# One inverse root of the norms for both halves of an image, and new places for the loop's steps, in a vision tower on Trainium2

## The chip, the cores and the metric

The kernel runs on one core of a Trainium2 chip. The metric is the device time of one execution in microseconds (us). The engines are TensorE (PE, with its weight loads as PEld), VectorE (DVE), ScalarE (ACT), GpSimd (POOL) and SyncE (SP), which here does nothing but issue DMA transfers. Each engine works through its own list of instructions strictly in order; between engines there are only semaphores.

## The reference, cut to what matters

Sixteen images of 3 x 256 x 256 go through three stages. A normalised 31 x 31 correlation gives 256 tokens of width 256 for each image, then comes causal attention and then a feed-forward part. The change lies in the attention:

```python
q = (x @ Wq).reshape(b, n, QH, DH).transpose(0, 2, 1, 3)        # QH = 16, DH = 64
k = kv[..., :H * DH].reshape(b, n, H, DH).transpose(0, 2, 1, 3) # H = 8
def _l2norm(x):
    n = jnp.maximum(jnp.linalg.norm(x, axis=-1, keepdims=True), 1e-12)
    return x / n
q = _mh_rmsnorm(q, q_gamma)       # _l2norm(q) * gamma
k = _mh_rmsnorm(k, k_gamma)
sim = jnp.einsum('bhgid,bhjd->bhgij', q, k)
sim = jnp.tanh(sim / SOFTCLAMP) * SOFTCLAMP * DH ** (-0.5)
attn = jax.nn.softmax(jnp.where(causal, neg, sim), axis=-1)
out = jnp.einsum('bhgij,bhjd->bhid', attn, v) @ Wout
```

So every token has 24 norms to be inverted in an image: 16 of queries and 8 of keys. A token sits in a partition; the 256 tokens of an image are two halves ("tb" 0 and 1) of 128.

## The kernel before

The three stages are three blocks, one after another, with a meeting of all engines between them: `token_stage`, `attention_stage`, `mlp_stage`. The attention works on 4 groups of 4 images (`GROUPS`, `GI`). Three groups are iterations of a loop in the program (`BODY`), the last is written out behind it (`FINAL`). The queries and keys of the very first image are made at the end of the token stage (`FIRST`, by `first_parts`), and each group makes those of the first image of the next group near its end (`EDGE_AT`).

The work of a group is a list of steps, `attention_order`. Each step has a place in a table, a number whose unit is one head: head n of the group's 32 has its score at place n. The list is sorted by place, and every engine takes from it, in that order, its own share of each step. The tables are `IMAGE_AT` (for an image, relative to the place at which its heads begin), `EDGE_AT`, `GROUP_AT` and the three constants under them. The steps that matter:

- **make** (0 to 7): one of eight projections of an image. PE does six matmuls into one of four PSUM banks (`job`); ACT copies queries and keys to `raw` (L924) and values to `v` (L928). 0 to 2 are the queries and keys of half 0, 4 to 6 of half 1; 3 and 7 are values.
- **square** (ACT, L936): squares the 1536 columns of a half into `squares`, which the profile calls `lines`. There is one such buffer, so the square of half 1 waits until the sum of half 0 has read it.
- **sum** (DVE, L990): 1536 squares to 24 norms in `rn`.
- **root** (DVE, L996 to L1011): clip, a first guess from the bits, three Newton steps of three instructions: eleven instructions on 128 x 24.
- **scale** (DVE, L1018): multiplies 1536 columns by the inverse norms.
- **turn** (0, 1, 2, 4, 5, 6): PE transposes scaled queries or keys (L1123), ACT writes the fp16 high part (L945, L949), and **low** is DVE's low part (L1027, L1032). A turn of half 0 waits for scale 0.
- **score** (PE L1136; ACT tanh L955 and exp L958; POOL mask L888). The tile `sim` holds one head, so the score of head n on PE waits for the tanh of head n-1 on ACT.
- **mix** (PE L1151, DVE L1040 to L1048), two heads and a half behind the score; **turn_o**, **project** and **norm** (DVE L1064 to L1080) end a group; **turn_h** and the **rms** steps prepare the tokens of the next group.
- **bits** (DVE, L1053): ORs a chunk of the feed-forward weights, `words`, 704 columns of int32, into `bits`, to learn which of two multiplication routes these weights allow. A group has eight chunks and two bits steps for each image. There is one buffer `words`: SP fetches the next chunk when the bits step of the last one is done.

SP's list in a group, in which every transfer stands behind the ones above it:

```python
sp.wait_ge(at.s_job, run.jobs_before(g))                       # BODY only
sp.dma_start(at.hn[:], rows(g + 1)).then_inc(at.s_hn, 16)      # lines<-tokens
for c in range(CHUNKS):
    if c == 1:
        sp.wait_ge(at.s_store, g * 32 + 32)
        sp.dma_start(h[:], rows(g)).then_inc(at.s_h, 16)
    sp.wait_ge(at.s_bits, g * CHUNKS + c + 1)
    sp.dma_start(at.words[:], WORDS[...]).then_inc(at.s_words, 16)
sp.wait_ge(at.s_x1, g + 1)                                     # after norm, BODY only
for half in range(2):
    sp.dma_start(X1[g * 2 + half], h[...]).then_inc(at.s_store, 16)
```

Of the kernel before, what the change touches and what calls it, by code (L numbers as in the profile page):

```python
# [8 lines left out]
I32 = mybir.dt.int32  # L9
ALU = mybir.AluOpType  # L10
# [29 lines left out]
ROOT_SEED = float(0x5F3759DF)  # L40
# [2 lines left out]
EPS_LN = 1e-5  # L43
W3 = QH * DH + 2 * HEADS * DH
QK = QH * DH + HEADS * DH
ROOTS = 1
BANKS = 4
WH = W3 // 2
WPARTS = [(half, f) for half in range(2) for f in range(FB)]
# [5 lines left out]
class Shared:  # L55


    def __init__(self, nc, ctx):
# [21 lines left out]
        def gone(name, shape, dt=F32):  # L80
            with nc.sbuf_tensor(name, shape, dt, side="right") as early:
                return early
# [18 lines left out]
        self.rn = sb("rn", [P, 2, QK // DH])  # L101
        self.guess = sb("guess_b", [P, ROOTS * (QK // DH)])
        self.slope = sb("slope_b", [P, ROOTS * (QK // DH)])
        sb("x_second_end", [P, plane - HEADS * TOK - (2 + 2 * ROOTS) * (QK // DH)])
        self.dump_first = gone("dump_first", [P, PR, D])
# [58 lines left out]
def token_stage(nc, sh, at, X, XT, TF, TPAD, H, WORDS, WEIGHTS, WQKV, NW, GQ, GK):  # L164
# [533 lines left out]
NH = GI * HEADS  # L698
LAG = 2
IMAGE_AT = {  # L700
    ("make", 0): -8, ("make", 1): -8, ("make", 2): -7.725, ("square", 0): -7.18, ("make", 6): -6.997,
    ("sum", 0): -6.79, ("root", 0): -6.361, ("make", 4): -6.348, ("scale", 0): -6.321, ("make", 5): -5.839,
    ("make", 3): -5.512, ("square", 1): -5.39, ("sum", 1): -5.219, ("turn", 0): -4.545, ("make", 7): -4.423,
    ("root", 1): -4.413, ("low", 0): -4.389, ("turn", 1): -3.147, ("scale", 1): -2.767, ("low", 1): -2.619,
    ("turn", 2): -2.538, ("low", 2): -1.89, ("turn", 4): -1.49, ("low", 4): -1.23, ("turn", 5): -1.205,
    ("turn", 6): -1.068, ("low", 5): -1.063, ("low", 6): -0.99,
}
EDGE_AT = {
    ("make", 0): -8, ("make", 1): -8, ("make", 2): -8, ("square", 0): -7.718, ("make", 6): -6.743,
    ("sum", 0): -6.311, ("make", 4): -5.808, ("root", 0): -5.602, ("scale", 0): -5.343, ("make", 5): -4.841,  # L710
    ("square", 1): -4.533, ("make", 3): -3.75, ("sum", 1): -3.523, ("root", 1): -2.958, ("make", 7): -2.776,
    ("scale", 1): -1.653, ("turn", 0): -0.263, ("low", 0): 0.74, ("turn", 1): 1.01, ("turn", 2): 2.113,
    ("low", 1): 2.862, ("low", 2): 3.052, ("turn", 4): 3.86, ("low", 4): 4.18, ("turn", 5): 4.291,
    ("turn", 6): 4.697, ("low", 5): 4.751, ("low", 6): 4.828,
}
GROUP_AT = {
    ("rms_sum", 0): 4, ("rms_sum", 1): 6, ("rms_sum", 2): 8.635, ("rms_sum", 3): 15.072, ("turn_h", 0): 19.823,
    ("turn_h", 1): 19.97, ("turn_h", 2): 20.742, ("turn_h", 3): 21.416, ("project", 0): 36.821,
    ("project", 1): 37.209, ("project", 2): 37.906, ("project", 3): 38,
}  # L720
GROUP_AT.update({("rms_root", 0): 15.489, ("rms_scale", 0): 16.649, ("norm", 0): 38.109})
MIX_AT, TURN_O_AT, BITS_AT = LAG + 0.502, (1.332, 2.286), (2.334, 7.379)


def first_parts():

    tokens = [("turn_h", k) for k in range(4)]
    makes = [("make", 0, j) for j in (0, 1, 2)] + [("square", 0, 0), ("sum", 0, 0), ("root", 0, 0)]
    makes += [("make", 0, j) for j in (4, 5, 6)] + [("square", 0, 1), ("scale", 0, 0), ("sum", 0, 1), ("root", 0, 1)]
    makes += [("make", 0, j) for j in (3, 7)] + [("scale", 0, 1)]  # L730
    turns = [[(kind, 0, 4 * tb + r) for r in range(3) for kind in ("turn", "low")] for tb in range(2)]
    return {"tokens": tokens, "makes": makes, "turns": turns}
# [57 lines left out]


FIRST_PARTS = first_parts()
FIRST = Stretch(FIRST_PARTS["tokens"] + FIRST_PARTS["makes"] + FIRST_PARTS["turns"][0] + FIRST_PARTS["turns"][1], False, 0)
BODY = Stretch(attention_order(False), True, 1)
# [10 lines left out]
class Attention:  # L805
# [162 lines left out]
    def vector_steps(self, dve, run, g, steps):  # L968
# [4 lines left out]
        for step in steps:  # L973
# [13 lines left out]
            elif kind == "sum":  # L987
                tb = step[2]
# [1 line left out]
                dve.reduce_sum(self.rn[:, tb], self.squares[:, 0:QK].rearrange("p (h d) -> p h d", d=DH), AX_X)\  # L990
                   .then_inc(self.s_ss, 1)
            elif kind == "root":
                tb = step[2]
                t = self.image(g, step[1]) * 2 + tb
                dve.wait_ge(self.s_ss, t + 2)
                dve.tensor_scalar(self.rn[:, tb], self.rn[:, tb], 1e-24, None, ALU.max).then_inc(self.s_clip, 1)  # L996
                dve.wait_ge(self.s_clip, t + 1)
                dve.tensor_scalar(self.guess[:].bitcast(I32), self.rn[:, tb].bitcast(I32), -0.5, ROOT_SEED,
                                  ALU.mult, ALU.add).then_inc(self.s_guess, 1)
                for k in range(NEWTON):  # L1000
                    dve.wait_ge(self.s_guess, t * NEWTON + k + 1)
                    dve.tensor_tensor(self.slope[:], self.guess[:], self.guess[:], ALU.mult).then_inc(self.s_slope, 1)
                    dve.wait_ge(self.s_slope, (t * NEWTON + k) * 2 + 1)
                    dve.scalar_tensor_tensor(out=self.slope[:], in0=self.slope[:], scalar=-0.5, in1=self.rn[:, tb],
                                             op0=ALU.mult, op1=ALU.mult).then_inc(self.s_slope, 1)
                    dve.wait_ge(self.s_slope, (t * NEWTON + k) * 2 + 2)
                    if k < NEWTON - 1:
                        dve.scalar_tensor_tensor(out=self.guess[:], in0=self.slope[:], scalar=1.5, in1=self.guess[:],
                                                 op0=ALU.add, op1=ALU.mult).then_inc(self.s_guess, 1)
                    else:  # L1010
                        dve.scalar_tensor_tensor(out=self.rn[:, tb], in0=self.slope[:], scalar=1.5, in1=self.guess[:],  # L1011
                                                 op0=ALU.add, op1=ALU.mult).then_inc(self.s_rn, 1)
            elif kind == "scale":
                tb = step[2]
                dve.wait_ge(self.s_rn, self.image(g, step[1]) * 2 + tb + 1)
                heads = self.raw[:, tb].rearrange("p (h d) -> p h d", d=DH)
                by = self.rn[:, tb].rearrange("p (h d) -> p h d", d=1).to_broadcast([P, QH + HEADS, DH])
                dve.tensor_tensor(heads, heads, by, ALU.mult).then_inc(self.s_qn, 1)  # L1018
            elif kind == "low":
                img, tb, r = step[1], step[2] // 4, step[2] % 4  # L1020
# [3 lines left out]
                if r < 2:  # L1024
                    for e in range(4):
                        u = 4 * r + e
                        ins = dve.scalar_tensor_tensor(out=self.q_lo[:, img % 2, u, cols], in0=bank[:, e * P:(e + 1) * P],  # L1027
                                                       scalar=self.gamma[:, u:u + 1], in1=self.q_hi[:, img % 2, u, cols],
                                                       op0=ALU.mult, op1=ALU.subtract)
                    ins.then_inc(self.s_emptied["queries"], 1)  # L1030
                else:
                    dve.scalar_tensor_tensor(out=self.k_lo[:, img % 2, :, cols], in0=bank.rearrange("p (h t) -> p h t", t=P),  # L1032
                                             scalar=KEY_SCALE, in1=self.k_hi[:, img % 2, :, cols],
# [659 lines left out]
```

## Time and profile before

| | |
|---|---|
| median of 3 runs | 1805.04 us (1791.48 to 1810.17) |
| profiled execution, its own time | 1788.73 us |
| its span | 1786.9 us |
| PE busy | 1726.3 us, 97% |
| DVE busy | 1137.2 us, 64% |
| ACT busy | 930.3 us, 52% |
| POOL busy | 427.8 us, 24% |

The span is from the first to the last instruction of the profiled execution; its own time has 1.8 us around that. The first and last of the three plain runs differ by 18.7 us, so a difference of about 1% is what a measurement of this kernel can tell from none. A busy share is an average over the three stages: the token stage ends at about 536 us of the span, the attention lies from 537 to 1112 us, and the feed-forward part follows. A clock column (PEclk) gives the clock granted to TensorE as a share of 2.4 GHz; 0.50 is 1.2 GHz.

### The profile page before, as it was taken

The page shows a single profiled execution, that of the slowest core. Times are in us where ns is not written, and L with a number is a line of the kernel's source. Part 1 is how long each engine was busy: PE and PEld are TensorE (multiplying, and loading weights), DVE is VectorE, ACT ScalarE, POOL GpSimd, SP SyncE. Part 2 cuts the span into 40 slices and gives each one's busy share as a digit, 9 for nine tenths or more (in the row PEclk, how much of TensorE's full clock was granted, in tenths as well). Part 3 has the DMA queues.
Part 4 walks back from the last instruction along what each step waited for, and adds up shares of the span by engine and source line. Part 5 has one row for each costly group of instructions (what it writes and reads, how often), then busy time and mean ns, then how long its engine had stood idle before and what let it go on. Part 6 is the DMA issues. An engine that isn't in the chain of part 4 may idle for free. (4 is left out here: it accounts for less than half of the span.)

```text
span 1786.9 us, 33009 instructions
## 1 busy us (share of the span) xinstructions
PE 1726.3 (97%) x12152; PEld 1509.7 (84%) x12152; DVE 1137.2 (64%) x2191; ACT 930.3 (52%) x1309; POOL 427.8 (24%) x515
## 2 busy tenths in 40 slices
PE   5999999999999999999999998999999999999998
PEld 5999998999987887888888887788888888888886
DVE  7899898898996877786877884423324141515242
ACT  8655555566658985895995994222222222222221
POOL 2000000000112222221222321434344333434343
PEclk9999999999999999999999999999999999999999
DMA  6322222223103002001100203600000000000000
GB/s 195 111 89 85 113 79 111 86 78 143 48 1 108 26 18 89 26 26 71 36 26 9 81 18 112 214 1 24 25 1 24 1 25 1 24 1 24 1 13 13
DMA packets 26421, 97.23 MB, mean 54 GB/s; under 512 B 3081, under 2 KB 11401, under 8 KB 21010
## 3 DMA queue, kind: packets, MB, share of 16 engines
q1 hardware_dynamic: 26258, 94.96, 15.5%
q8 instruction: 115, 1.88, 0.4%
q14 instruction: 48, 0.39, 0.1%
HBM read 82.33 MB, written 24.15 MB: 60 GB/s over the span
## 5 line engine op out<-in xcount | busy, mean ns | idle before, releaser
L658 PE MATMUL conv<-w,x 128*128 128x368 f16 (+5 forms) x3960 | 452.7, 277 | 3.8 <-issue 3.8
L658 PEld LDWEIGHTS conv<-w,x 128*128 128x128 f16 x3960 | 427.2, 146 | 27.9 <-issue 4.5
L1439 ACT ACTIVATE raw_c<-ring,sh 128x512 f32<-128x512 f32 x128 | 87.6, 689 | 334.3 <-PE ring L1542 334.2
L1451 DVE CAST ha_hi<-raw_c 128x512 fp32r<-128x512 f32 x128 | 85.2, 665 | 201.0 <-ACT raw_c L1439 198.8
L888 POOL TENSOR_SCALAR_AFFINE_SELECT probs<-probs 128x256 f32<-128x256 f32 x256 | 129.9, 530 | 342.2 <-ACT probs L958 342.2
L1398 POOL TENSOR_TENSOR ha_lo<-raw_c,ha_hi 128x512 fp32r<-128x512 f32 x128 | 165.3, 1291 | 189.5 <-DVE ha_hi L1451 189.5
L1542 PE MATMUL ring<-ha_hi,wh 128*128 128x512 f32 x512 | 199.4, 389 | 0.9 <-POOL ha_lo L1398 0.9
L1542 PE MATMUL ring<-ha_lo,wh 128*128 128x512 f32 x512 | 199.2, 389 | 0.0
L1542 PE MATMUL ring<-hb_lo,wh 128*128 128x512 f32 x512 | 199.2, 389 | 0.0
L1542 PE MATMUL ring<-hb_hi,wh 128*128 128x512 f32 x512 | 199.2, 389 | 0.0
L1151 PEld LDWEIGHTS mixed<-v,probs 128*128 128x128 f32 x1536 | 185.5, 193 | 10.7 <-POOL probs L888 1.7
L1151 PE MATMUL mixed<-v,probs 128*128 128x65 f32 x1536 | 192.2, 275 | 1.9 <-DVE o L1044 1.8
L1451 DVE CAST hb_hi<-raw_c 128x512 fp32r<-128x512 f32 x64 | 35.7, 558 | 187.3 <-ACT raw_c L1439 187.0
L379 ACT ACTIVATE lines<-job 128x512 f32<-128x512 f32 x96 | 50.0, 605 | 167.8 <-PE job L638 167.7
L955 ACT ACTIVATE probs<-sim,span 128x768 f32<-128x768 f32 x128 | 115.8, 905 | 12.6 <-PE sim L1136 12.0
L472 DVE TENSOR_TENSOR_SCAN box<-lines 128x271 f32<-128x271 f32 x192 | 120.2, 699 | 3.5 <-ACT lines L379 3.5
L1114 PE MATMUL job<-wqkv_hi,ht_hi 128*128 128x512 f32 x256 | 110.5, 432 | 7.6 <-PEq L171 3.6
L1398 POOL TENSOR_TENSOR hb_lo<-raw_c,hb_hi 128x512 fp32r<-128x512 f32 x64 | 82.5, 1290 | 140.5 <-DVE hb_hi L1451 140.5
L1542 PEld LDWEIGHTS ring<-ha_hi,wh 128*128 128x128 f32 x512 | 96.1, 188 | 21.6 <-POOL ha_lo L1398 1.6
L1542 PEld LDWEIGHTS ring<-hb_lo,wh 128*128 128x128 f32 x512 | 96.1, 188 | 20.0
L1542 PEld LDWEIGHTS ring<-ha_lo,wh 128*128 128x128 f32 x512 | 96.1, 188 | 19.9
L1542 PEld LDWEIGHTS ring<-hb_hi,wh 128*128 128x128 f32 x512 | 96.1, 188 | 19.9
(161 smaller groups left out, 3198.5 us busy)
## 6 DMA issues: line engine op xcount, KB each, us to landing
xt<-x_columns_in SPq DMA_DIRECT2D x12, 1163.0 KB, 5.2
xp<-x_patches_in SPq DMA_DIRECT2D x12, 1152.0 KB, 5.1
hidden_words<-hidden_weights_in SPq DMA_DIRECT2D x8, 1408.0 KB, 8.5
words<-hidden_words SPq DMA_DIRECT2D x32, 352.0 KB, 3.0
wh<-hidden_words SPq DMA_DIRECT2D x8, 1024.0 KB, 10.0
tokens<-planes SPq DMA_DIRECT2D x4, 1024.0 KB, 4.6
h<-tokens SPq DMA_DIRECT2D x4, 1024.0 KB, 7.3
attended<-h SPq DMA_DIRECT2D x8, 512.0 KB, 3.5
```

The costliest lines, as they stand in the source:

```text
L379: act.activation(dst, turn[:, k % 4], ACT.Copy).then_inc(s_across, 1)
L472: return dve.tensor_tensor_scan(out, line[:, TH:TH + SCAN], line[:, 0:SCAN], 0.0, ALU.add, ALU.subtract)
L658: ins = pe.matmul(out, xs[:, c, RI - 1 - i:RI - 1 - i + NR, :, x].rearrange("p r g -> p (r g)"), w, start=(t == 0), stop=(t == size - 1), ...
L888: ins = pool.affine_select(out=diag, in_=diag, compare_op=ALU.is_ge, fill=0.0, base=0, pattern=[[0, 2], [1, P]], channel_multiplier=-1)
L955: act.activation(self.probs[:, n % 4], self.sim[:, :, 0:3 * P], ACT.Tanh, scale=self.span[:, 2:3]).then_inc(self.s_tanh, 1)
L1114: ins = pe.matmul(bank, x[:, f, img % GI, P * tb:P * tb + P], w[:, f, 512 * r:512 * r + 512], start=(t == 0), stop=(t == len(terms) - 1))
L1151: ins = pe.matmul(out, self.probs[:, n % 4, m, at:at + P], self.v[:, img % 2, jb, 2 * (hd // 2) + m], start=(jb == 0), stop=(jb == ib), sk ...
L1398: pool.tensor_tensor(dst[1][:, u % KH], raw[:, u % 4], dst[0][:, u % KH].bitcast(F32), ALU.subtract).then_inc(s_lo, 1)
L1439: act.activation(raw[:, u % 4], bank, ACT.Gelu, scale=scale[:, m:m + 1]).then_inc(s_gelu, 1)
L1451: dve.tensor_copy(dst[0][:, u % KH], raw[:, u % 4]).then_inc(s_hi, 1)
L1542: ins = pe.matmul(bank, a, b, start=start, stop=False, skip_group_check=True)
```

## The change

Two things are changed. First, the root is taken once for an image, on 48 norms, after the sums of both halves, where it was taken twice on 24. `guess` and `slope` are twice as wide (`ROOTS = 2`), `scale` of either half waits for that one root, and the two columns of `rn` are read as one. Second, the tables of places are new, as is the order in `first_parts`.

```diff
-ROOTS = 1
+ROOTS = 2
...
 IMAGE_AT = {
...
-    ("sum", 0): -6.79, ("root", 0): -6.361, ("make", 4): -6.348, ("scale", 0): -6.321, ("make", 5): -5.839,
...
+    ("make", 3): -5.898, ("root", 0): -5.788, ("make", 7): -5.749, ("scale", 0): -5.689, ("scale", 1): -4.382,
...
-MIX_AT, TURN_O_AT, BITS_AT = LAG + 0.502, (1.332, 2.286), (2.334, 7.379)
+MIX_AT, TURN_O_AT, BITS_AT = LAG + 0.95, (2.679, 3), (0.625, 1.427)
...
-    makes = [("make", 0, j) for j in (0, 1, 2)] + [("square", 0, 0), ("sum", 0, 0), ("root", 0, 0)]
-    makes += [("make", 0, j) for j in (4, 5, 6)] + [("square", 0, 1), ("scale", 0, 0), ("sum", 0, 1), ("root", 0, 1)]
+    makes = [("make", 0, j) for j in (0, 1, 2)] + [("square", 0, 0), ("sum", 0, 0)]
+    makes += [("make", 0, j) for j in (4, 5, 6)] + [("square", 0, 1), ("sum", 0, 1), ("root", 0, 0), ("scale", 0, 0)]
...
             elif kind == "root":
-                tb = step[2]
-                t = self.image(g, step[1]) * 2 + tb
-                dve.wait_ge(self.s_ss, t + 2)
-                dve.tensor_scalar(self.rn[:, tb], self.rn[:, tb], 1e-24, None, ALU.max).then_inc(self.s_clip, 1)
+                t = self.image(g, step[1])
+                norms = self.rn[:].rearrange("p b h -> p (b h)")
+                dve.wait_ge(self.s_ss, 2 * t + 3)
+                dve.tensor_scalar(norms, norms, 1e-24, None, ALU.max).then_inc(self.s_clip, 1)
...
             elif kind == "scale":
                 tb = step[2]
-                dve.wait_ge(self.s_rn, self.image(g, step[1]) * 2 + tb + 1)
+                dve.wait_ge(self.s_rn, self.image(g, step[1]) + 1)
```

The two bits steps of an image stood at 2.334 and 7.379 behind the start of its heads, and now stand at 0.625 and 1.427. Three places show what becomes of the lists.

On DVE, from the norm that ends a group (L1080) into the next group, before. In a row, `b_words` is the semaphore of a landed chunk, `b_sq` of a square, `b_ss` of a sum, `b_rn` of a root, `b_mix` of a mix on PE.

```order
L1080 TENSOR_SCALAR h<-h,moments_b,rstd_b 128x256 x7
...
L990 TENSOR_REDUCE rn<-lines 128x24 [waits b_sq]
L996 TENSOR_SCALAR rn<-rn 128x24 [waits b_ss]
L998 TENSOR_SCALAR guess_b<-rn 128x24 [waits b_clip]
...
L1011 SCALAR_TENSOR_TENSOR rn<-slope_b,guess_b 128x24 [waits b_slope]
L1018 TENSOR_TENSOR raw<-raw,rn 128x1536 [waits b_rn]
L1053 TENSOR_TENSOR bits<-bits,words 128x704 [waits b_bits,b_words]
L1040 RECIPROCAL rl<-mixed 128x4 [waits b_mix]
```

The same place on DVE now.

```order
L1080 TENSOR_SCALAR h<-h,moments_b,rstd_b 128x256 x7
...
L1053 TENSOR_TENSOR bits<-bits,words 128x704 [waits b_bits,b_words]
L990 TENSOR_REDUCE rn<-lines 128x24 [waits b_sq]
L1053 TENSOR_TENSOR bits<-bits,words 128x704 [waits b_bits,b_words]
L990 TENSOR_REDUCE rn<-lines 128x24 [waits b_sq]
L996 TENSOR_SCALAR rn<-rn 128x48 [waits b_ss]
...
L1011 SCALAR_TENSOR_TENSOR rn<-slope_b,guess_b 128x48 [waits b_slope]
L1018 TENSOR_TENSOR raw<-raw,rn 128x1536 [waits b_rn]
L1040 RECIPROCAL rl<-mixed 128x4 [waits b_mix]
```

The first bits step moved from behind the first scale to the very front, ahead of the first sum; the second, which stood five heads later, is between the two sums.

On ACT, at the start of a group, from the first square to the tanh of the fourth head, before. L924 and L928 are the copies of makes, `b_emptied_act` counts them.

```order
L936 ACTIVATE lines<-raw 128x1536 [waits b_ss,b_emptied_act]
L955 ACTIVATE probs<-sim,span 128x768 [waits b_mix,b_score]
L958 ACTIVATE probs<-probs 128x768 [waits b_tanh]
L924 ACTIVATE raw<-job 128x512 [waits b_job] x2
L955 ACTIVATE probs<-sim,span 128x768 [waits b_mix,b_score]
L958 ACTIVATE probs<-probs 128x768 [waits b_tanh]
L924 ACTIVATE raw<-job 128x512 [waits b_job]
L928 ACTIVATE v<-job 128x8x64 [waits b_mix,b_job]
L936 ACTIVATE lines<-raw 128x1536 [waits b_ss,b_emptied_act]
L955 ACTIVATE probs<-sim,span 128x768 [waits b_mix,b_score]
```

The same place on ACT now.

```order
L936 ACTIVATE lines<-raw 128x1536 [waits b_ss,b_emptied_act]
L955 ACTIVATE probs<-sim,span 128x768 [waits b_mix,b_score]
L958 ACTIVATE probs<-probs 128x768 [waits b_tanh]
L924 ACTIVATE raw<-job 128x512 [waits b_job] x3
L936 ACTIVATE lines<-raw 128x1536 [waits b_ss,b_emptied_act]
L955 ACTIVATE probs<-sim,span 128x768 [waits b_mix,b_score]
L958 ACTIVATE probs<-probs 128x768 [waits b_tanh]
L928 ACTIVATE v<-job 128x8x64 [waits b_mix,b_job] x2
```

The second square moved ahead of the tanh of the third head; before it stood ahead of that of the fourth.

On PE, behind the first mix of a group, now. `b_qn` is the semaphore of a scale.

```order
L1151 MATMUL mixed<-v,probs 128x65 [waits b_mixread,b_mask]
...
L1136 MATMUL sim<-q_hi,k_hi 128x256 [waits b_tanh]
...
L1151 MATMUL mixed<-v,probs 128x65 [waits b_mixread,b_mask]
...
L1136 MATMUL sim<-q_hi,k_hi 128x256 [waits b_tanh]
...
L1123 MATMUL job<-ident,raw 128x128 [waits b_qn,b_emptied_act]
```

All eight makes and three scores now stand ahead of this first mix, and the first turn behind the score of the fifth head; before, seven makes and three scores stood ahead of it, and the first turn behind the score of the fourth head, with one make still to come.

## Rows read from the trace of the kernel before

**Rows 1.** Busy time by stretch: start:end, length, PE, PEld, DVE, ACT, POOL, PEclk.

```profile
541.00:1106.00 565.00, 550.87 (x4561) 469.93 (x4560) 424.05 (x1140) 451.43 (x768) 142.14 (x269) 0.99 0.14 47
696.00:716.00 20.00, 18.65 (x161) 16.42 (x159) 16.99 (x46) 17.34 (x40) 5.92 (x10) 0.83 0.31 115
```

**Rows 2.** Waits of PE, 541 to 1106: total us, times, longest.

```profile
PE mixed L1151 <- DVE o L1044: 1.8, 2, 1.4
```

**Rows 3.** Groups of DVE, 541 to 1106: count, busy us, mean ns, idle before.

```profile
L1018 DVE TENSOR_TENSOR raw<-raw,rn 128x1536 f32<-128x1536 f32 x30 | 53.3, 1777 | 0.4
L990 DVE TENSOR_REDUCE rn<-lines 128x24 f32<-128x1536 f32 x30 | 52.5, 1749 | 16.6 <-ACT lines L936 16.4
L1053 DVE TENSOR_TENSOR bits<-bits,words 128x704 int32<-128x704 int32 x32 | 30.9, 964 | 3.6 <-DMA words<-hidden_words 3.6
...
L1002 DVE TENSOR_TENSOR slope_b<-guess_b 128x24 f32<-128x24 f32 x90 | 17.3, 193 | 3.1
```

**Rows 4.** Timeline of PE, second group: start us, length us, idle before.

```profile
683.99 0.50 PE L1114 MATMUL job<-wqkv_hi,ht_hi 128*128 128x512 f32 x1 [0.96 <-DVE h L1064]
...
696.14 1.45 PE L1151 MATMUL mixed<-v,probs 128*128 128x65 f32 x12
...
699.88 0.48 PE L1114 MATMUL job<-wqkv_hi,ht_hi 128*128 128x512 f32 x1
...
701.45 0.28 PE L1136 MATMUL sim<-q_hi,k_hi 64*128 64x256 f16 x2
...
702.04 1.55 PE L1151 MATMUL mixed<-v,probs 128*128 128x65 f32 x12
...
708.51 2.79 PE L1151 MATMUL mixed<-v,probs 128*128 128x65 f32 x12 [1.35 <-DVE o L1044]
```

**Rows 5.** Timeline of DVE at the start of the second group.

```profile
687.59 2.77 DVE L1080 TENSOR_SCALAR h<-h,moments_b,rstd_b 128x256 f32<-128x256 f32 x8 [2.25 <-POOL rstd_b L896]
...
700.02 0.89 DVE L1053 TENSOR_TENSOR bits<-bits,words 128x704 int32<-128x704 int32 x1 [2.21 <-DMA words<-hidden_words]
```

**Rows 6.** Timeline of SP's DMA issues at the start of the second group.

```profile
692.15 0.35 SPq L1192 DMA_DIRECT2D lines<-tokens  x1
692.90 0.59 SPq L1198 DMA_DIRECT2D words<-hidden_words  x1
695.10 0.33 SPq L1196 DMA_DIRECT2D h<-tokens  x1
701.08 0.33 SPq L1198 DMA_DIRECT2D words<-hidden_words  x1
```

**Rows 7.** Tile words, the chunk issued at 701.1: issue to landing, us.

```profile
DMA to landing us min/median/max: 3.1/3.1/3.1
```

**Rows 8.** Timeline of ACT, second group: the second square and the tanh behind it.

```profile
696.92 1.48 ACT L936 ACTIVATE lines<-raw 128x1536 f32<-128x1536 f32 x1
698.31 0.90 ACT L955 ACTIVATE probs<-sim,span 128x768 f32<-128x768 f32 x1
```

**Rows 9.** Timeline of PE, the first make of the third group.

```profile
833.23 0.49 PE L1114 MATMUL job<-wqkv_hi,ht_hi 128*128 128x512 f32 x1 [0.96 <-DVE h L1064]
```

**Rows 10.** Timeline of DVE, the first bits step of the third group.

```profile
848.44 0.89 DVE L1053 TENSOR_TENSOR bits<-bits,words 128x704 int32<-128x704 int32 x1 [1.36 <-DMA words<-hidden_words]
```

**Rows 11.** Timeline of PE, the first make of the last group.

```profile
978.75 0.47 PE L1114 MATMUL job<-wqkv_hi,ht_hi 128*128 128x512 f32 x1 [0.83 <-issue]
```

**Rows 12.** Tile words, 986.0 to 987.5: the last group's first chunk.

```profile
L1198 SPq DMA_DIRECT2D words<-hidden_words x1: 557/557/557, 986.6 to 986.6; - x1
...
DMA to landing us min/median/max: 4.4/4.4/4.4
```

**Rows 13.** Tile words, 542 to 543: the first group's first chunk.

```profile
L1198 SPq DMA_DIRECT2D words<-hidden_words x1: 347/347/347, 542.3 to 542.3; - x1
...
DMA to landing us min/median/max: 5.2/5.2/5.2
```

**Rows 14.** Timeline of PE, the first mix of the first group.

```profile
551.46 1.45 PE L1151 MATMUL mixed<-v,probs 128*128 128x65 f32 x12
```

More of the change, by code:

```diff
@@ L700 @@
 IMAGE_AT = {
-    ("make", 0): -8, ("make", 1): -8, ("make", 2): -7.725, ("square", 0): -7.18, ("make", 6): -6.997,
-    ("sum", 0): -6.79, ("root", 0): -6.361, ("make", 4): -6.348, ("scale", 0): -6.321, ("make", 5): -5.839,
-    ("make", 3): -5.512, ("square", 1): -5.39, ("sum", 1): -5.219, ("turn", 0): -4.545, ("make", 7): -4.423,
-    ("root", 1): -4.413, ("low", 0): -4.389, ("turn", 1): -3.147, ("scale", 1): -2.767, ("low", 1): -2.619,
-    ("turn", 2): -2.538, ("low", 2): -1.89, ("turn", 4): -1.49, ("low", 4): -1.23, ("turn", 5): -1.205,
@@ L706 @@
-    ("turn", 6): -1.068, ("low", 5): -1.063, ("low", 6): -0.99,
+    ("make", 0): -8, ("make", 2): -8, ("make", 1): -7.639, ("square", 0): -7.258, ("sum", 0): -7.065,
+    ("make", 6): -6.738, ("make", 4): -6.591, ("make", 5): -6.54, ("square", 1): -6.092, ("sum", 1): -5.91,
+    ("make", 3): -5.898, ("root", 0): -5.788, ("make", 7): -5.749, ("scale", 0): -5.689, ("scale", 1): -4.382,
+    ("turn", 0): -3.293, ("turn", 1): -3.106, ("low", 0): -3.002, ("low", 1): -2.585, ("turn", 2): -2.355,
+    ("turn", 4): -1.801, ("low", 2): -1.411, ("turn", 5): -1.099, ("turn", 6): -1.007, ("low", 4): -0.728,
@@ L707 @@
+    ("low", 5): -0.393, ("low", 6): -0.2,
 }
 EDGE_AT = {
[L709 to L713, printed above, removed]
@@ L714 @@
-    ("turn", 6): 4.697, ("low", 5): 4.751, ("low", 6): 4.828,
+    ("make", 0): -8, ("make", 1): -8, ("make", 6): -8, ("make", 2): -6.838, ("square", 0): -6.773, ("sum", 0): -6.15,
+    ("make", 4): -5.871, ("make", 5): -5.426, ("square", 1): -5.408, ("sum", 1): -4.903, ("root", 0): -4.559,
+    ("make", 3): -4.296, ("scale", 0): -3.515, ("make", 7): -2.169, ("scale", 1): -2.126, ("turn", 0): -0.473,
+    ("turn", 1): 1.494, ("low", 0): 1.678, ("low", 1): 2.558, ("turn", 2): 3.339, ("low", 2): 3.65,
@@ L715 @@
+    ("turn", 4): 4.546, ("low", 4): 4.554, ("turn", 5): 4.868, ("low", 5): 5.007, ("turn", 6): 5.041,
+    ("low", 6): 5.165,
 }
 GROUP_AT = {
-    ("rms_sum", 0): 4, ("rms_sum", 1): 6, ("rms_sum", 2): 8.635, ("rms_sum", 3): 15.072, ("turn_h", 0): 19.823,
-    ("turn_h", 1): 19.97, ("turn_h", 2): 20.742, ("turn_h", 3): 21.416, ("project", 0): 36.821,
-    ("project", 1): 37.209, ("project", 2): 37.906, ("project", 3): 38,
-}
-GROUP_AT.update({("rms_root", 0): 15.489, ("rms_scale", 0): 16.649, ("norm", 0): 38.109})
@@ L722 @@
-MIX_AT, TURN_O_AT, BITS_AT = LAG + 0.502, (1.332, 2.286), (2.334, 7.379)
+    ("rms_sum", 0): 3.791, ("rms_sum", 1): 8.365, ("rms_sum", 2): 9.606, ("rms_sum", 3): 15.392,
+    ("turn_h", 0): 18.316, ("turn_h", 1): 18.429, ("turn_h", 2): 20.558, ("turn_h", 3): 21.624,
+    ("project", 0): 37.164, ("project", 1): 37.193, ("project", 2): 37.217, ("project", 3): 38,
+}
+GROUP_AT.update({("rms_root", 0): 15.642, ("rms_scale", 0): 16.459, ("norm", 0): 38.343})
+MIX_AT, TURN_O_AT, BITS_AT = LAG + 0.95, (2.679, 3), (0.625, 1.427)
@@ L992, in vector_steps @@
             elif kind == "root":
-                tb = step[2]
-                t = self.image(g, step[1]) * 2 + tb
-                dve.wait_ge(self.s_ss, t + 2)
-                dve.tensor_scalar(self.rn[:, tb], self.rn[:, tb], 1e-24, None, ALU.max).then_inc(self.s_clip, 1)
+                t = self.image(g, step[1])
+                norms = self.rn[:].rearrange("p b h -> p (b h)")
+                dve.wait_ge(self.s_ss, 2 * t + 3)
+                dve.tensor_scalar(norms, norms, 1e-24, None, ALU.max).then_inc(self.s_clip, 1)
                 dve.wait_ge(self.s_clip, t + 1)
-                dve.tensor_scalar(self.guess[:].bitcast(I32), self.rn[:, tb].bitcast(I32), -0.5, ROOT_SEED,
+                dve.tensor_scalar(self.guess[:].bitcast(I32), norms.bitcast(I32), -0.5, ROOT_SEED,
                                   ALU.mult, ALU.add).then_inc(self.s_guess, 1)
@@ L1003, in vector_steps @@
                     dve.wait_ge(self.s_slope, (t * NEWTON + k) * 2 + 1)
-                    dve.scalar_tensor_tensor(out=self.slope[:], in0=self.slope[:], scalar=-0.5, in1=self.rn[:, tb],
+                    dve.scalar_tensor_tensor(out=self.slope[:], in0=self.slope[:], scalar=-0.5, in1=norms,
                                              op0=ALU.mult, op1=ALU.mult).then_inc(self.s_slope, 1)
@@ L1010, in vector_steps @@
                     else:
-                        dve.scalar_tensor_tensor(out=self.rn[:, tb], in0=self.slope[:], scalar=1.5, in1=self.guess[:],
+                        dve.scalar_tensor_tensor(out=norms, in0=self.slope[:], scalar=1.5, in1=self.guess[:],
                                                  op0=ALU.add, op1=ALU.mult).then_inc(self.s_rn, 1)
```

## The prediction

> **What bounds the kernel now.** I read the busy shares by stretch first, then the waits of PE, then the timelines where a group begins. In the attention, the only stage whose lists change much, PE is busy 550.87 of 565 us [rows 1]: 14.1 us of idle time is all that an order can win there. PE is the bound; DVE (424) and ACT (451) have slack on average. What the tables decide is whether some list makes PE wait. PE's waits for mixes add up to 1.8 us [rows 2], nearly all of it one wait of 1.35 us at 708.51 [rows 4]; the twelve matmuls behind it take 2.79 us where the same twelve took 1.45 to 1.55, and the clock in the 20 us around is 0.83 of full speed [rows 1]: it fell to its lower level, 1.2 GHz, once PE had been idle. That cost 0.17 x 20 = 3.4 us more.
>
> Now look at DVE when the second group begins. It ends the norm at 687.59 + 2.77 = 690.36 and starts its first bits step at 700.02, after 2.21 us of idle time that a DMA ended [rows 5]. SP issues the chunk at 692.90, directly behind the 1 MB of tokens for the next group, and both behind the stores that the norm releases [rows 6]. So the chunk is there 9.5 us after the norm, and the old order had put a sum, a root and a scale between, so only 2.2 us were lost. The third group repeats it with 1.36 us [rows 10]. All bits steps together waited 3.6 us [rows 3].
>
> **The root.** It is off PE's path except through the turns. Sixteen images lose eleven instructions on 24 columns of about 0.19 us and a gap, 3.1 us of gaps in 90 being 0.03 each [rows 3]: 11 x 0.22 = 2.4 us, 38 us over the kernel. The 48-column ones cost more; no row shows that width. From below the extra is nothing, from above double; 24 columns at the rate of the sum (1536 columns in 1749 ns, 1.14 ns each [rows 3]) is 27 ns, so 0.3 us a root, 2.7 us in all. DVE gains 38 - 5 = 33 us. Of itself that moves PE by nothing: PE waits for DVE in few places. For scale 0 it is even a delay, since it now needs the sum of half 1 as well. In the token stage the one root ends before the second scale did, with PE at its correlations: nothing.
>
> **The bits steps.** This is where I expect the time to go. In the new list DVE comes from the norm straight to bits 0, then sum 0, then bits 1, sum 1, root, scale 0. Behind the waiting DVE stand: sum 0; on ACT, square 1 (one buffer `squares`) and, queued behind it, the tanh of the third head; on PE, the score of the fourth head, which waits for that tanh.
>
> The second group. PE starts at 683.99 and had done seven makes and three scores by 696.14 [rows 4]. Now it does a mix (1.4) and the eighth make before the fourth score (699.88 to 701.45, 1.6): it arrives at 699.1. DVE: bits 0 from 700.0 to 700.9, sum 0 (1.75) to 702.6; ACT: square 1 (1.48) to 704.1, tanh (0.90) to 705.0 [rows 3, 5, 8]. **PE idles 5.9 us.** Then bits 1: its chunk is issued at 701.08 and lands 3.1 us later, 704.2 [rows 6, 7]. Bits 1 to 705.2, sum 1 to 706.9, root 2.7 to 709.6, scale 0 (1.78) to 711.3. PE's list reaches turn 0 a score (0.6), a mix (1.4) and a score behind the first wait, which without any wait is 701.7. **It can start it at 711.3: 9.6 us lost in all**, the 5.9 among them. DVE then has mixes and lows in hand, of 0.6 to 1.1 us each, against a make, a turn or a mix of PE for each; I find no further wait.
>
> The third group. Its PE starts 149.24 later (833.23 [rows 9]), its bits step 148.42 later (848.44 [rows 10]); with the same chain of 11.3 us behind the landing, scale 0 ends at 859.7 and PE arrives at 850.9: 8.8 us.
>
> The last group has no tokens to fetch. Its chunk is issued at 986.6 and lands at 991.0 [rows 12]; bits 0 ends at 991.9. Chunk 1 goes out at once, behind the 1 MB for `h`, so I give it the 4.4 us of [rows 12]: 996.5. Then 0.9 + 1.75 + 2.7 + 1.78: 1003.6. PE arrives 17.7 after 978.75 [rows 11], 996.5: 7.1 us.
>
> The first group has no norm before it. Chunk 0 lands at 542.3 + 5.2 = 547.5 [rows 13], bits 0 ends at 548.5, chunk 1 is there 3.1 later, 551.7; the chain ends at 558.8. PE's first mix stood at 551.46 [rows 14], so turn 0 falls due 5.5 later (701.7 - 696.14), at 557.0: 1.8 us.
>
> Sum: 9.6 + 8.8 + 7.1 + 1.8 = 27.3. Off it go the waits of the old order that these replace, 1.8 [rows 2] and 3.4 of clock, and 1 for small waits that a lighter DVE may end, out of the 12.3 us of idle time that remain. Most of these stand at the end of a group, where PE's order is the same in both kernels. On top comes clock: the fall at 708.51 followed 1.35 us of idle time, and there will be four longer ones. Bounds are 0 and 4 x 3.4 = 13.6, and part of slow work lies inside a wait for scale 0 anyway; I take 4. **+25 us.**
>
> **Inside a group** the two bits steps of an image are 0.8 of a head apart, with sum 0 (1.75) and a mix (0.6) between them, and a chunk needs 3.1 us. The wait of up to 0.8 us lies before sum 1, which stands still for square 1 anyway, and that one for make 5 on PE. By the lengths above turn 0 has about a microsecond to spare. If not, it is up to 0.8 in each of 12 images: +9.6, an end of the range.
>
> **A rule weighed.** The chunk took 7.0 us from its issue at 692.90 to the bits step at 700.0 behind a megabyte [rows 5, 6], and 3.1 alone [rows 7]. The Trainium skill ("DMA: Bandwidth & Descriptors", section "Queues, rings and completion order") says that one engine's transfers use one ring on each DMA engine and are taken up in ring order, and that a semaphore's increment lands after all earlier writes. By that rule a chunk behind a megabyte cannot be early, the trace agrees, and the first wait stands. The page also says that the data of a later transfer may be finished before an earlier one's, but that does not free a waiter.
>
> **Rivals.**
> - *A chunk that waits for nobody* (0.17). If the chunks came 3.1 us after issue, at 696.0 for the second group, the waits of the three later groups shrink by about 4, 4 and 1.5 us: +25 - 9.5 = +15. Against it stands the 7.0 us above. For it: the smaller burst if the norm ends earlier.
> - *DVE's relief wins* (0.12). The 33 us that DVE gains take away the waits for mixes, the fall of the clock at 708 and some of the rest: 1.8 + 3.4 + 3 = -8 us, 1797. It needs the chunk landed before DVE is due. To be in time for PE's fourth score at 699.1, DVE would have to start bits 0 at 699.1 - 0.9 - 1.5 - 1.75 - 0.9 = 694.0; the chunk comes at 699.9. That is the point on which it decides, 6 us away. Even with every idle microsecond and the 3.4 gone, the gain is 17.5 us, under 1%.
> - *More than the forecast* (0.13). The clock falls in each group, +10, and the waits inside a group show, +10: +45.
> - That the change does not do what it says is ruled out by the lists.
>
> **How the numbers follow.** The profiled execution took 1788.73 us, 1.8 more than its span; with +25 it would be 1813.7, 1.4% more. The median of the plain runs, 1805.04, is 16 us above the profiled one, for a reason that no row shows, so I add 25 to it: **1830**. The forecast, +15 to +40, has 0.58. The range reaches from the second rival's upper part (+3, with runs that lie 9 below their median) to +47: 1799 to 1852. About 1% is what a measurement tells from no change, 18 us. Slower by more: 0.13, 0.50 of the forecast's 0.58 and a little of the first rival, 0.65. Within 1%: 0.32. Faster by more: 0.03, since the rows allow 17.5.
>
> **What would show it.** In the changed profile DVE's idle time before L1053, ended by a DMA, rises from 3.6 us to 20 or more, with waits of about 9.5 us right behind the norm in the second and third group and 5.5 in the last. PE waits for ACT's tanh at the fourth score (about 6, 5 and 2 us) and for L1018 at the first turn. The root's instructions number 16 x 11, each near 0.22 us. Feed-forward and token stage are as long as before. It is wrong if PE's idle time in the attention stays near 14 us: then the chunk lands sooner than I think, or DVE reaches it later.

## The result and the profile after

The changed kernel takes 1856.93 us in the median (4 runs, 1854.8 to 1863.0), the kernel before 1805.07 (1791.48 to 1810.17): a ratio of 1.032, with an interval of 1.0266 to 1.0375. The forecast was 1830 and its range ended at 1852. The sign was right and the size was not: 52 us instead of 25. Between the two profiled executions it is even 69.9 us (1858.62 against 1788.73). One slow run of the kernel before, 2183.93 us, stands beside four of the experiments below and is left out of their ratios.

Busy time by stretch in the changed kernel comes first: the attention, the starts of its second, third and last group, and its end. The columns are those of [rows 1].

```profile
541.00:1182.00 641.00, 601.88 (x4585) 517.59 (x4585) 407.89 (x991) 450.19 (x768) 132.57 (x269) 0.90 0.13 43
700.00:740.00 40.00, 32.09 (x217) 27.92 (x212) 21.97 (x51) 22.77 (x45) 6.76 (x14) 0.70 0.26 88
862.00:907.00 45.00, 37.99 (x225) 32.43 (x224) 22.24 (x52) 24.53 (x48) 5.36 (x14) 0.62 0.20 71
1030.00:1057.00 27.00, 20.60 (x153) 18.26 (x153) 18.02 (x48) 17.81 (x33) 5.99 (x12) 0.68 0.13 43
1120.00:1170.00 50.00, 47.16 (x256) 41.48 (x257) 13.96 (x36) 18.35 (x21) 7.45 (x19) 0.52 0.20 74
```

Two things grew. PE's idle time is 641 - 601.9 = 39 us where [rows 1] has 14, or 36 without the 3 us at the end of the stretch, a wait between two stages that both kernels have and that lies behind the end of the stretch of [rows 1]. And the clock: 0.99 over the attention before, 0.90 now. In the last row PE is busy 47 of 50 us and runs at 0.52: it waits for 3 us there and is slow through all the rest. That row was in no term of mine.

The waits of the attention that bear on this, longest first: who waited, for whom, total us, times, longest.

```profile
...
DVE bits L1053 <- DMA words<-hidden_words: 47.9, 15, 10.0
...
DVE rn L990 <- ACT lines L936: 36.7, 14, 8.4
...
ACT lines L936 <- DVE rn L990: 19.2, 3, 8.2
...
PE sim L1136 <- ACT probs L955: 15.9, 9, 6.3
...
PE job L1123 <- DVE raw L1018: 8.9, 4, 3.6
```

Read from above they are one chain: DVE waits for the chunk (3.6 us before [rows 3], 47.9 now), ACT's square for DVE's sum, PE's score for the tanh behind that square. DVE at the start of the second group, where [rows 5] had 2.21 us:

```profile
693.07 2.77 DVE L1080 TENSOR_SCALAR h<-h,moments_b,rstd_b 128x256 f32<-128x256 f32 x8 [2.25 <-POOL rstd_b L896]
705.85 0.89 DVE L1053 TENSOR_TENSOR bits<-bits,words 128x704 int32<-128x704 int32 x1 [10.01 <-DMA words<-hidden_words]
706.66 1.75 DVE L990 TENSOR_REDUCE rn<-lines 128x24 f32<-128x1536 f32 x1
710.12 0.89 DVE L1053 TENSOR_TENSOR bits<-bits,words 128x704 int32<-128x704 int32 x1 [1.72 <-DMA words<-hidden_words]
...
713.16 0.21 DVE L1002 TENSOR_TENSOR slope_b<-guess_b 128x48 f32<-128x48 f32 x1
```

And PE there, beside [rows 4]:

```profile
703.02 1.45 PE L1151 MATMUL mixed<-v,probs 128*128 128x65 f32 x12
710.76 0.40 PE L1136 MATMUL sim<-q_hi,k_hi 64*128 64x256 f16 x2 [6.29 <-ACT probs L955]
...
711.83 2.82 PE L1151 MATMUL mixed<-v,probs 128*128 128x65 f32 x12
...
717.35 1.97 PE L1123 MATMUL job<-ident,raw 128*128 128x128 f32 x8 [1.62 <-DVE raw L1018]
719.11 2.66 PE L1151 MATMUL mixed<-v,probs 128*128 128x65 f32 x12
```

The wait is where it was forecast and as long (5.9 forecast, 6.29 measured). Behind it the same twelve matmuls take 2.82 us instead of 1.45: the lower clock level, 1.2 GHz. The records of the granted clock have it from 707.1 to 731.0, from 867.5 to 901.7, from 1034.8 to 1051.9 and from 1120.1 to 1167.9. Each of the four falls lies in a wait of PE.

### The profile page after: what moved, and what is told of

The parts are those of the page before. It is cut to its first block and busy times, and to the rows that moved or that the text cites. A ratio compares the mean times of both kernels' runs of the same rounds, so it can differ in the third digit from the quotient of the medians.

```text
span 1856.9 us, 32737 instructions
## 1 busy us (share of the span) xinstructions
PE 1772.8 (95%) x12152; PEld 1553.3 (84%) x12152; DVE 1115.0 (60%) x2015; ACT 928.6 (50%) x1309; POOL 418.6 (23%) x515
## 5 line engine op out<-in xcount | busy, mean ns | idle before, releaser
L1151 PEld LDWEIGHTS mixed<-v,probs 128*128 128x128 f32 x1536 | 209.8, 214 | 6.9 <-issue 1.8
L1151 PE MATMUL mixed<-v,probs 128*128 128x65 f32 x1536 | 213.6, 295 | 0.0
L888 POOL TENSOR_SCALAR_AFFINE_SELECT probs<-probs 128x256 f32<-128x256 f32 x256 | 120.9, 495 | 410.5 <-ACT probs L958 410.4
L1114 PE MATMUL job<-wqkv_hi,ht_hi 128*128 128x512 f32 x256 | 109.0, 426 | 7.7 <-PEq L171 3.6
## 6 DMA issues: line engine op xcount, KB each, us to landing
wh<-hidden_words SPq DMA_DIRECT2D x8, 1024.0 KB, 10.2
```

What stands on the lines that cost most here:

```text
L888: ins = pool.affine_select(out=diag, in_=diag, compare_op=ALU.is_ge, fill=0.0, base=0, pattern=[[0, 2], [1, P]], channel_multiplier=-1)
L1114: ins = pe.matmul(bank, x[:, f, img % GI, P * tb:P * tb + P], w[:, f, 512 * r:512 * r + 512], start=(t == 0), stop=(t == len(terms) - 1))
L1151: ins = pe.matmul(out, self.probs[:, n % 4, m, at:at + P], self.v[:, img % 2, jb, 2 * (hd // 2) + m], start=(jb == 0), stop=(jb == ib), sk ...
```

## The experiments

Fifteen runs. Theory A: DVE waits for chunks at the new places of the bits steps, and PE idles behind it. Theory B: the single root and the other new places cost it. Theory C: much of the time goes at the low clock that follows a wait, and is more than the wait.

**Bits steps back.** The changed kernel, with only

```diff
-MIX_AT, TURN_O_AT, BITS_AT = LAG + 0.95, (2.679, 3), (0.625, 1.427)
+MIX_AT, TURN_O_AT, BITS_AT = LAG + 0.95, (2.679, 3), (2.334, 7.379)
```

> The changed kernel with the two bits steps of an image back at 2.334 and 7.379; all else as changed. Theory A (the bits steps make DVE wait, PE idles, and its clock falls after that): DVE's idle time before the bits step falls from 47.9 us to under 5, PE's idle time in the attention from 36 to 14 to 20 us, and the time comes back to 1790 to 1812. Theory B (the single root behind both sums and the crowded makes are what costs): PE still waits for the scale at each group's first turn and the time stays above 1835.

Measured: 1823.88 us (9 runs), 1.0099 of before (1.0067 to 1.0130). DVE waits for no chunk at all, and 33 of the 52 us are gone. Theory A holds for these; but the time did not come down to 1812, so something else of the change costs some 17 us (1807.00 for the kernel before in the runs beside it). PE's waits in the attention of this kernel, of those that differ:

```profile
PE job L1123 <- DVE raw L1018: 4.8, 4, 1.2
PE job L1123 <- DVE ht_lo L985: 4.7, 6, 0.8
...
PE mixed L1151 <- DVE o L1044: 2.9, 7, 0.6
...
PE sim L1136 <- DVE k_lo L1032: 2.3, 1, 2.3
```

The first row is 1.2 us at the first turn of each group, for a scale 0 that now needs both sums. The last is the one wait at head 24 of the last group, 2.3 us instead of 1.2, of which more below.

**Bits steps alone.** The kernel before, with only

```diff
-MIX_AT, TURN_O_AT, BITS_AT = LAG + 0.502, (1.332, 2.286), (2.334, 7.379)
+MIX_AT, TURN_O_AT, BITS_AT = LAG + 0.502, (1.332, 2.286), (0.625, 1.427)
```

> The kernel before with nothing but the two bits steps moved to 0.625 and 1.427. Theory A: the chunk is waited for right behind the norm as in the changed kernel; here the first turn stands one score earlier in PE's list, so its wait is the long one (7 to 10 us in the second and third group); the clock falls behind it and the time is 1840 to 1870. Theory B: 1795 to 1815, as before.

Measured: 1861.98 us, 1.0292 of before (1.0222 to 1.0362). One line in the old tables does as much harm as the whole change. As expected the wait sits at the first turn here:

```profile
DVE bits L1053 <- DMA words<-hidden_words: 62.3, 17, 9.7
...
PE job L1123 <- DVE raw L1018: 34.1, 4, 11.5
```

**Which of the two steps.** The second step back to 7.379, with the first left at 0.625:

> The changed kernel with only the second bits step moved back to 7.379. Theory A in detail: the first wait stays (PE idle about 6, 5 and 2 us at the fourth score); scale 0 of the second group ends about 1 us earlier (bits 1, 0.9 us, is gone from its chain, its chunk had landed 0 to 2 us late), in the last group 4 us earlier; the time is 1835 to 1855. If the second step was the costly one, it is under 1820.

Measured: 1849.69 us, 1.026 of before (1.0193 to 1.0327). And the second left early, but the first chunk of a group issued before the norm of the group ahead:

```diff
+            def chunk(k):
+                sp.wait_ge(at.s_bits, k + 1)
+                sp.dma_start(at.words[:], WORDS[:, bass.ds(k * CW, CW)].bitcast(I32)).then_inc(at.s_words, 16)
+            chunk(0)
...
-                for c in range(CHUNKS):
+                for c in range(1, CHUNKS):
...
+                    chunk(g * CHUNKS + c)
+                if run is BODY:
+                    chunk(g * CHUNKS + CHUNKS)
```

> The changed kernel with only the first chunk of a group issued early, before the norm of the group ahead. Theory A in detail: the wait at the fourth score goes (14 us to under 1), but the second chunk is now asked for at once behind the norm and stands behind stores, tokens and h in the ring, so scale 0 is hardly earlier and the first turn waits 7 to 9 us in the second and third group instead of 2: idle time of PE falls by less than 6 us in all. Time 1835 to 1855. If the first step alone was the cause, it is under 1815.

Measured: 1851.78 us, 1.027 of before (1.0203 to 1.0337). By itself either gives little, 7 and 5 us against the changed kernel. In the second of the two the wait moved as expected from the score to the turn, though PE's idle time in the attention rose by 3 us where I had said it would fall a little:

```profile
PE job L1123 <- DVE raw L1018: 25.6, 4, 8.5
...
PE sim L1136 <- ACT probs L955: 1.9, 5, 0.4
```

Its DVE shows why. The first bits step waits for nothing, and the second then waits for the chunk that stands behind the stores, the tokens and `h`:

```profile
699.09 0.89 DVE L1053 TENSOR_TENSOR bits<-bits,words 128x704 int32<-128x704 int32 x1 [0.34 <-issue]
700.06 1.75 DVE L990 TENSOR_REDUCE rn<-lines 128x24 f32<-128x1536 f32 x1
711.57 0.89 DVE L1053 TENSOR_TENSOR bits<-bits,words 128x704 int32<-128x704 int32 x1 [9.76 <-DMA words<-hidden_words]
```

**Both of them:**

> The changed kernel with the second bits step at 7.379 and with SP issuing the first chunk of a group before the norm of the group ahead instead of behind its stores and the tokens. Theory A: no bits step waits any more (under 3 us on DVE), the wait at the fourth score goes from 14 us to about 0, at the first turn about 1 us a group stays, and the time is 1785 to 1810. Theory B: above 1835.

Measured: 1813.86 us (10 runs, 1804.51 to 1820.79), 1.007 of before (1.0031 to 1.0109). The long waits are gone and 43 of the 52 us with them, where the two halves alone gave 7 and 5. DVE's waits for chunks are 11.9 us and not under 3, 6.2 of it at the very start of the attention, and PE waits for none of that.

**The root alone.** The kernel before with one root, and the root and scale 0 placed right behind the second sum, every other place as it was (`EDGE_AT` is changed in the same way):

```diff
-    ("sum", 0): -6.79, ("root", 0): -6.361, ("make", 4): -6.348, ("scale", 0): -6.321, ("make", 5): -5.839,
-    ("make", 3): -5.512, ("square", 1): -5.39, ("sum", 1): -5.219, ("turn", 0): -4.545, ("make", 7): -4.423,
+    ("sum", 0): -6.79, ("make", 4): -6.348, ("make", 5): -5.839,
+    ("make", 3): -5.512, ("square", 1): -5.39, ("sum", 1): -5.219, ("root", 0): -5.2, ("scale", 0): -5.19,
+    ("turn", 0): -4.545, ("make", 7): -4.423,
```

> The kernel before with one root for both halves, put right behind the second sum, and scale 0 behind it; every other place as before. DVE's busy time falls by about 33 us. Theory A: no gain that shows; the first turn, which stands early in the old list, now waits for the second sum (2 to 5 us in each of 16 images), so 1805 to 1850. Theory B says the same with a larger part of the change's 52 us here. Were the root worth something alone, it would be 1780 to 1795.

Measured: 1912.68 us, 1.0614 of before (1.0547 to 1.0681), far outside every expectation. PE waits at a first turn in twelve images:

```profile
PE job L1123 <- DVE raw L1018: 79.1, 12, 8.5
```

So the saving of the root is no saving with the old places: 104 us more than the 1808.27 beside it. The other new places, with the first turn later than before, bring that down to the +17 of the first experiment, not to zero. Which of them does it was not tested.

**Keeping PE at work where it waits.** Into the changed kernel's list of PE go transposes that nobody reads, into a bank that PE owns at that moment:

```diff
+FILL = {(False, ("score", 3)): 44, (False, ("turn", 1, 0)): 14, (True, ("score", 3)): 20, (True, ("turn", 1, 0)): 30}
...
+        def fill(run, step, into):
+            for _ in range(FILL.get((run is FINAL, step), 0)):
+                pe.transpose(into, self.ident[:], self.ident[:])
...
+                fill(run, step, bank[:, 0:P])
                 pe.wait_ge(self.s_qn, self.image(g, img) * 2 + tb + 1)
...
+                if (run is FINAL, step) in FILL:
+                    pe.wait_ge(self.s_mixread, g * NH + n - 1)
+                    fill(run, step, self.mixed[:, n % 2, 0:P])
```

> The changed kernel with transposes of a constant tile put into PE's list where it waits: 44 (about 4.8 us) before the fourth score and 14 before the first turn of each looped group, 20 and 30 in the last. They add work to PE and take no wait away. If the low clock is what the waits cost beyond themselves (theory C), PE's clock stays at its upper level behind the group starts, some 20 us come back although PE has 20 us more to do, and the time is 1825 to 1845; the fall at 1120, which has no filler, stays. If the low clock comes from something else than idle time, or was hidden, the time is 1860 to 1870.

Measured: 1830.77 us, 1.0124 of before (1.0052 to 1.0197): more work, 26 us less time. DVE still waits 49.9 us for chunks. The 224 transposes take 27.5 us of PE, and yet its busy time in the whole kernel is 4 us shorter than without them: the rest of its work runs 31 us faster. The first two rows below are the starts of the second and third group, which ran at 0.70 and 0.62 without the filler; the third is the end of the attention, which has none.

```profile
700.00:740.00 40.00, 38.05 (x309) 33.47 (x308) 22.25 (x52) 27.45 (x54) 6.67 (x16) 0.91 0.34 115
860.00:905.00 45.00, 41.63 (x363) 36.56 (x361) 30.64 (x70) 32.70 (x62) 7.85 (x18) 1.00 0.23 79
1100.00:1150.00 50.00, 46.04 (x268) 40.78 (x268) 15.87 (x42) 20.10 (x24) 8.12 (x19) 0.59 0.20 74
```

The same with 12 more transposes before the score of head 24 in the last group, `(True, ("score", 24)): 12`:

> As the kernel with fillers, and 12 more transposes (1.3 us) before the score of head 24 in the last group, where PE waited 1.45 us for the last low part and the clock then stayed low for 47.8 us. Theory C: that stretch runs at the upper clock, and the time is 15 to 24 us under that of the kernel with fillers at the group starts alone. If the fall has nothing to do with the wait, no difference.

Measured: 1824.39 us, 6.4 under the last, less than the 15 expected. The clock in the same last stretch is 0.93, so that part did what it should. But its third group had 10 us at the low clock that the kernel without had not, and the 1830.77 is the middle of two pairs of runs: 1836 and 1837 us with a mean granted clock of 0.98, and 1820 and 1825 with 0.99. Two of those four seem to have been without the long stretch already.

```profile
860.00:905.00 45.00, 41.99 (x325) 36.90 (x324) 27.18 (x59) 30.76 (x59) 6.64 (x16) 0.89 0.22 72
1100.00:1150.00 50.00, 44.19 (x356) 38.91 (x354) 23.66 (x67) 23.85 (x34) 9.83 (x23) 0.93 0.20 74
```

**That filler alone**, first in the kernel before, then in the changed one:

> The kernel before with nothing but 12 transposes of a constant tile (1.3 us) before the score of head 24 in the last group, where PE waits 1.2 us for the last low part. The plain runs of the kernel before fall in two clusters, near 1790 and near 1808 us, and only the profile of one near 1790 is known. Theory C: the upper cluster is the executions in which the clock falls at that wait and stays low to the end of the attention, so with the filler nearly all runs lie at 1783 to 1797, median near 1790. If the clusters have another cause, they stay and the median is near 1807.

Measured: 1793.93 us, all five runs from 1793.7 to 1797.0, while nine runs of the kernel before beside it lie from 1789.5 to 1808.6, with 1802.06 in the middle. The ratio is 0.9971 (0.9929 to 1.0012), which doesn't tell it from the kernel before; what is clear is the spread. The upper cluster is gone, at the price of 1.3 us of filler.

> The changed kernel with nothing but the filler before score 24. Theory C: the last 48 us at the low clock go and with them 14 to 24 us: 1832 to 1843. What then stays above the kernel before with the same filler is the share of the group starts, 40 to 52 us. If that stretch was there for another reason, 1855 to 1860.

Measured: 1843.9 us, 1.0233 of before (1.0188 to 1.0278), 13 less than the changed kernel and 1 short of what was expected. With that stretch out of both, the changed kernel is 50 us slower, against 52 with it: the end of the attention is hardly a part of the difference of the medians.

**The kernel before, profiled three times more:**

> The kernel before, unchanged, profiled once more. If its time is near 1808, its records show the clock low from the wait for the last low part (about 1070) to about 1112, some 40 us, where the first profile (1788.7) showed none; near 1790 they show none.

Measured: 1807.87, 1805.88 and 1796.62 us. The first two show the clock low for 44.4 and 47.8 us to the end of the attention, the third for only 6.8 us there. The wait for the last low part is the same in all of them: 1.18, 1.18 and 1.19 us here, 1.19 in the first profile of this kernel. The first of the three, at the end of the attention, and the instruction with the wait:

```profile
1071.00:1116.00 45.00, 41.49 (x241) 36.68 (x242) 13.55 (x35) 18.80 (x22) 7.43 (x19) 0.53 0.26 90
```

```profile
1071.79 0.28 PE L1136 MATMUL sim<-q_hi,k_hi 64*128 64x256 f16 x2 [1.18 <-DVE k_lo L1032]
```

In the same profile the clock came back inside the output projection (L1172), the 64 matmuls of 256 columns that start at 1112.3:

```profile
1112.00:1118.00 6.00, 5.68 (x14) 4.59 (x15) 0.00 (x0) 0.22 (x1) 0.00 (x0) 0.51 0.00 0
1118.00:1129.00 11.00, 11.00 (x52) 9.45 (x50) 4.33 (x9) 0.00 (x0) 0.00 (x0) 1.00 0.00 0
```

This profile also is the fair partner of the changed kernel's, since both have the long stretch. PE's busy time in the whole kernel, of the changed kernel first, then of this profile, then of the changed kernel with its bits steps back:

```profile
PE 1772.8 (95%) x12152; PEld 1553.3 (84%) x12152; DVE 1115.0 (60%) x2015; ACT 928.6 (50%) x1309; POOL 418.6 (23%) x515
PE 1746.0 (97%) x12152; PEld 1525.3 (84%) x12152; DVE 1136.5 (63%) x2191; ACT 930.6 (52%) x1309; POOL 427.7 (24%) x515
PE 1746.4 (96%) x12152; PEld 1530.6 (84%) x12152; DVE 1110.5 (61%) x2015; ACT 929.0 (51%) x1309; POOL 426.4 (23%) x515
```

The spans are 1856.9, 1806.2 and 1818.1 us. So of the 50.7 us between the first two, 26.8 are the same matmuls taking longer and 23.9 are idle time of PE. Of the 11.9 us between the last two, all but 0.4 is idle time.

For the second and the third profile there stood:

> The same kernel again, with the same expectation: a time near 1808 goes with a long stretch at the low clock at the end of the attention, a time near 1790 with none.

> The same kernel again, with the same expectation: a time near 1808 goes with a long stretch at the low clock at the end of the attention, a time near 1790 with none.

**In search of a faster one.** The changed kernel mended in both ways, with the filler before head 24; and the kernel before with the filler and the early first chunk.

> The changed kernel with the first chunk early, the second bits step at 7.379, and the filler before score 24. Theory A and C together: the 47 us at the low clock at the end of the attention go, 18 to 24 us, and the time is 1788 to 1800. If the long stretch at the low clock has nothing to do with the wait, 1805 to 1820 as without the filler.

Measured: 1796.06 us, 0.9989 of before (0.9943 to 1.0036), 18 under the same kernel without the filler and no different from the kernel before. Its slowest run, the profiled one with 1807.45 us, has 20.5 us at the low clock elsewhere, behind the wait of 1.2 us at the first turn of the last group:

```profile
1001.00:1022.00 21.00, 20.79 (x113) 18.72 (x114) 13.42 (x37) 11.38 (x25) 4.92 (x10) 0.51 0.07 19
```

> The kernel before with the filler before score 24 and with the first chunk of a group issued before the norm. It takes away the 2.2 and 1.4 us for which DVE waited for a chunk, PE's wait of 1.35 us at 708 and the clock's fall behind it: 3 to 6 us under the kernel before with the filler alone, 1780 to 1792. If the early chunk is worth nothing, the same as that kernel.

Measured: 1788.43 us, 0.9939 of before (0.9897 to 0.9982), the fastest of all and 5.5 us under the kernel before with the filler alone. No bits step waits, and the stretch that stood at 0.83 in [rows 1] is clean:

```profile
700.00:720.00 20.00, 20.00 (x184) 16.99 (x184) 15.84 (x47) 19.40 (x46) 4.73 (x12) 1.00 0.14 43
```

## Why the prediction was wrong

- **What bounds the kernel.** PE, and what the tables decide is where it waits: right.
- **The root.** Right in size: an instruction takes 223 ns on 48 columns on the mean against 190 on 24, 33 ns more where 27 were put in. All root instructions together fell from 66.9 to 39.2 us, and the gaps between them from 11.2 to 6.4: 32.5 of the 33 us forecast. DVE's busy time in the whole kernel fell by 22 us, since other instructions got longer by some 5. But "moves PE by nothing" missed 1.2 us at the first turn of each group, seen once the bits steps are back, and the longer wait before head 24.
- **The bits steps.** The chain stands as it was put. At the fourth score 5.9 us were forecast in the second group and 6.29 came; in all four groups score and turn waits were put at 27.3 us and are 22.9 (14.0 at scores, 8.9 at turns), probably since a PE at half its clock arrives later. The bits steps alone, moved in the old tables, give the same loss, and taking both causes away gives 43 us back.
- **Inside a group** DVE waits up to 1.1 us for a chunk, and PE for none of it: right.
- **The rule weighed.** It held as far as it was needed: a chunk behind other transfers lands late. In the changed kernel it landed 7.4 us after its issue, 0.9 us behind the tokens issued just ahead of it. Whether the order of the queue holds it back, or only that the transfers share the same bandwidth, no run tells apart. The kernel with the first chunk early, with 9.76 us at its second bits step, shows that asking for one chunk early only passes the delay on to the next. The first rival had 15 us by a chunk that waits for nobody, and falls.
- **The step that failed: "Bounds are 0 and 4 x 3.4 = 13.6 ... I take 4."** The clock term was sized by the one fall in the trace of before, which lasted 6.8 us, and its upper bound by the thought that four falls cost four times that one. In the changed kernel the falls lasted 23.9, 34.1 and 17.1 us at the group starts and 47.8 at the end, 129 us at the low clock in the attention against 10. Of the 69.9 us between the profiles PE's idle time explains 36.2 - 14.1 = 22, close to the 24.5 that the forecast had for it (27.3 - 1.8 - 1); about 48 are clock. Against the profile of before with the long stretch, the clock is 26.8 us of 50.7: twice the upper bound. The filler shows that this is cause and not company: 27.5 us of matmuls put into the waits, and 26 us less time. The third rival, "the clock falls in each group, +10", had the mechanism and a third of the size; its other +10, waits inside a group, did not come.
- **The base.** "For a reason that no row shows" was the other warning. The profile of before was one of the executions that keep the high clock at the end of the attention; of its 42 runs on record 15 are under 1800 us. The others lose some 17 us there. So, it seems, do all four of the changed kernel's: their mean granted clocks are 0.958 to 0.965, with 0.962 for the profiled one that has the stretch. So some 17 of the 70 us between the profiles belong to neither kernel's tables, and the 52 between the medians are 22 to 24 of waits and 27 to 30 of clock at the group starts. That the forecast was built on the median, and not on the profile, was right; the reason was not known.
- Of the 52 us, the bits steps hold 33 (the run with the bits steps back). The rest, 17, is the single root with its new places. In the profiles it is 12 us, all of it idle time of PE; in the attention that is 23.6 us against 14.1 in the first profile of before. The 5 us up to 17 are in no profile. Which of the other places costs how much was not separated.

## What to carry to other kernels

Before a step is moved forward in a list, look at what it waits for, and where that transfer stands in its queue: a chunk asked for behind a burst of stores and loads is as late as the burst, however early its consumer is called. A cheap step at the head of an in-order engine's list can stop the engine that is the bound, through others that never mention it. And price a wait of TensorE by what its clock does afterwards, over several executions: here a microsecond of waiting cost 17 us or nothing. Filling the waits with matmuls that nobody reads gave back 26 us where taking the waits away gave 43, so it is the remedy for a wait that can't be taken away.

## What the runs showed of the hardware

The low clock can last far longer than the idle time before it. After 1.18 us without work PE ran at 0.53 for 44.4 us, while it was busy 41.5 of 45 us in mixes, scores and projections; in another execution of the same program the same wait was followed by no long fall.

The length does not follow the wait. The fall around 6.29 us of idle time lasted 23.9 us, one around 4.96 lasted 34.1. In the kernel with the root alone twelve waits of PE, 6.1 to 8.5 us each, have a fall each: eleven of them lasted 10.2 us, part of it still in the wait, and the twelfth 27.3.

What PE had to do behind the wait differs with the length. In those eleven a make (L1114, 512 columns) follows soon behind the wait, and the clock rose during it or within 2.5 us of its end. At the group starts of the changed kernel all eight makes of the image are done before the wait, and scores, turns and mixes follow; the stretches last 17 to 34 us. At the end of the attention there are only scores, mixes and a few transposes, and all nine profiles with a long stretch there (41.0 to 47.8 us) have its end 3 to 6 us into the output projection. But the twelfth fall of the kernel with the root alone had the same make behind it and lasted on. No run changed only the kind of work, so what ends a stretch stays open.

Twelve transposes, 1.3 us, in place of the 1.2 us wait made five executions agree within 3.3 us where those without them spread over 19.
